# One subtraction issued a place earlier on VectorE, and four GpSimd operations behind one more wait, in the 512-step scan of a four-phase kernel

## What is computed

```
i_couple = tanh(q) @ coupling.T
dq = q - q ** 3 / 3.0 - p + drive + i_couple + bias
dp = EPSILON * (q + ALPHA - BETA * p)
dq1, dp1 = _derivative(q, p, ...)
dq2, dp2 = _derivative(q + 0.5 * DT * dq1, p + 0.5 * DT * dp1, ...)
dq3, dp3 = _derivative(q + 0.5 * DT * dq2, p + 0.5 * DT * dp2, ...)
dq4, dp4 = _derivative(q + DT * dq3, p + DT * dp3, ...)
q_next = clip(q + DT / 6.0 * (dq1 + 2 * dq2 + 2 * dq3 + dq4))
p_next = clip(p + DT / 6.0 * (dp1 + 2 * dp2 + 2 * dp3 + dp4))
```

## Time and profile before

| | |
|---|---|
| median of 3 runs | 5410.8 us (5400.78 to 5411.15) |
| profiled execution, its own time | 5413.09 us |
| its span, first to last instruction | 5411.5 us |
| mean granted TensorE clock over the span | 0.712 |
| TensorE products busy | 4425.1 us (82%) |
| VectorE busy | 4190.9 us (77%) |
| ScalarE busy | 2313.5 us (43%) |
| GpSimd busy | 1674.5 us (31%) |
| scan: first clip of q to the last | 45.67 to 2891.76 us |

### The profile page before, as it was taken

How to read it: one execution, slowest core, us unless ns; L and a number is a source line. 1 busy time by engine, 2 the same in 40 slices (tenths; PEclk the granted TensorE clock), 3 DMA queues, 4 the chain that set the end, 5 groups by cost and what they waited for, 6 DMA issues and landing times. The chain is left out here.

```text
span 5411.5 us, 212004 instructions
## 1 busy us (share of the span) xinstructions
PE 4425.1 (82%) x78665; PEld 3826.1 (71%) x78665; DVE 4190.9 (77%) x25454; ACT 2313.5 (43%) x10538; POOL 1674.5 (31%) x5965
## 2 busy tenths in 40 slices
PE   6977777777777777777776878699999999879899
PEld 5966666666666666666665666587777787668777
DVE  8999999999999999999995667677777777631123
ACT  3343333333333333333333656555555555432243
POOL 2444444444444444444443222223332222100000
PEclk5555555555555555555556999799999999989999
DMA  2000000000000000000002010222222222141121
GB/s 95 27 1 1 1 1 1 1 1 1 1 1 1 1 1 1 1 1 1 1 1 80 9 44 17 87 75 67 86 86 78 82 75 68 34 148 39 52 90 39
DMA packets 147685, 188.32 MB, mean 35 GB/s; under 512 B 9148, under 2 KB 79364, under 8 KB 147112
## 3 DMA queue, kind: packets, MB, share of 16 engines
q1 hardware_dynamic: 145712, 182.66, 10.2%
q0 software_dynamic: 624, 0.75, 0.1%
q10 hardware_dynamic: 904, 0.15, 0.0%
HBM read 143.66 MB, written 39.90 MB: 34 GB/s over the span
## 5 line engine op out<-in xcount | busy, mean ns | idle before, releaser
L249 PE MATMUL bank<-tanh_parts,w_lo 128*128 128x4 f16 x32768 | 1208.4, 169 | 679.3 <-ACT tanh_parts L189 679.3
L249 PEld LDWEIGHTS bank<-tanh_parts,w_lo 128*128 128x128 f16 x32768 | 1035.4, 105 | 855.2 <-ACT tanh_parts L189 853.9
L189 ACT ACTIVATE tanh_parts<-ys 128x8 f16<-128x8 f32 x4096 | 861.6, 210 | 1760.4 <-DVE ys L347 1760.4
L257 PE MATMUL bank<-tanh_parts,w_hi 128*128 128x8 f16 x32768 | 1212.6, 173 | 2.0 <-issue 2.0
L257 PEld LDWEIGHTS bank<-tanh_parts,w_hi 128*128 128x128 f16 x32768 | 1066.4, 104 | 7.7 <-issue 2.1
L347 DVE TENSOR_TENSOR_SCAN ys<-mix,bank 128x24 f32<-128x24 f32 x4096 | 820.8, 202 | 105.7 <-PE bank L257 2.2
L190 ACT ACTIVATE tanh_full<-ys 128x8 f32<-128x8 f32 x4096 | 805.0, 197 | 0.0
L337 DVE TENSOR_TENSOR tanh_parts<-tanh_full,tanh_parts 128x8 f16<-128x8 f32 x4096 | 679.5, 166 | 1.6 <-ACT tanh_full L190 1.6
L1246 POOL TENSOR_TENSOR t_w_qk<-t_raw_qk,t_w_qk 128x512 fp32r<-128x512 f32 x128 | 168.0, 1334 | 710.1 <-ACT t_w_qk L1410 710.1
L515 PE MATMUL t_bank<-t_x,t_w_qk 128*128 128x512 f32 x1536 | 360.9, 391 | 12.8 <-DVE t_x L1666 12.8
L515 PEld LDWEIGHTS t_bank<-t_x,t_w_qk 128*128 128x128 f32 x1536 | 289.6, 189 | 73.8 <-DVE t_x L1666 13.5
(11 more groups left out here) (232 smaller groups left out, 9143.4 us busy)
## 6 DMA issues: line engine op xcount, KB each, us to landing
t_raw_qk<-L_cond_qkv_w_dram SPq DMA_DIRECT2D x128, 256.0 KB, 3.3
t_raw_vo<-L_cond_qkv_w_dram SPq DMA_DIRECT2D x16, 1024.0 KB, 5.2
t_raw_vo<-L_cond_out_w_dram SPq DMA_DIRECT2D x16, 1024.0 KB, 5.2
n<-t_parts SPq DMA_DIRECT2D x14, 1024.0 KB, 6.6
g_raw<-L_cond_ffn_w_dram SPq DMA_DIRECT2D x8, 1024.0 KB, 10.1
g_x<-n SPq DMA_DIRECT2D x8, 1024.0 KB, 11.8
xT<-L_cond_ada_w_dram SPq DMA_DIRECT2D x8, 768.0 KB, 5.4
t_x<-n SPq DMA_DIRECT2D x6, 1024.0 KB, 7.0
```

The costliest lines, as they stand in the source:

```text
L189: act.activation(tanh_parts[:, u, at, :, 0], ys[:, s, at, :, 2], ACT.Tanh, scale=1.0 / SCALE).then_inc(s_th, 1)
L249: pe.matmul(sums[:, :, 2], w_lo[:, w_of, k, m * P:(m + 1) * P], tanh_parts[:, u, k, :, 0], start=(m % 2 == 0 and k == 0), stop=False, skip ...
L257: last = pe.matmul(sums[:, :, 1:3], w_hi[:, w_of, k, m * P:(m + 1) * P], tanh_parts[:, u, k], start=False, stop=(m % 2 == 1 and k == C - 1 ...
```

## The change

VectorE's low part of half 1 in the last stage is issued in front of `slope` in place of behind it. GpSimd gets one more wait in front of the first of its four operations: beside the clip of q it waits for the rate of stage 0. No instruction that computes is added or taken away.

```diff
@@ -424,8 +424,8 @@
                 own("rate_3", stt(rate[:, 3], ps_[:, 3], -BETA, y3))
                 cubed(y3, GAIN[3])
                 low_part(t, 3, 0)
+                low_part(t, 3, 1)
                 sloped(y3, THIRD + GAIN[3])
-                low_part(t, 3, 1)
                 v.wait_ge(s_psum, t + 1)
                 own("moved", stt(p_new[:, :, :], rate[:, 3], EPSILON * H / 3, p_sum[:, :, :]))
                 after("slope")
@@ -475,6 +475,7 @@
                 g.wait_ge(s_p, t + 1)
                 tt(net[:, :, :], drive_now[:, :, :], p[:, :, :], ALU.subtract).then_inc(s_net, 1)
                 g.wait_ge(s_clip, t + 1)
+                g.wait_ge(s_rate, t * 3 + 1)
                 own(tt(gq[:, 0], q[:, :, :], by_rest, ALU.mult))
                 g.wait_ge(s_net, t + 1)
                 of_net = own(tt(gq[:, 1], net[:, :, :], by_third_h, ALU.mult))
```

## The result

The changed kernel takes **5361.4 us** (median of 4 runs, 5358.1 to 5365.6), the kernel before 5411.0 beside it (4 runs). The ratio is 0.9913, with a 95% interval of 0.9896 to 0.993: 50 us, or 0.9%, faster. Forecast were 5357 us and a range of 5338 to 5390.

What follows compares the result with a forecast made beforehand. No engine's busy time was the bound; waits between engines were, costing time in stages 3 and 0. Gains averaging 0.105 us per step over 512 steps, 54 us, gave 5357 us, range 5338 to 5390.

Steps and rivals of the forecast that it cites:

- The two places: Stages 3 and 0 of a step, said to lose 0.09 and 0.06 us against stage 2 before the first scan.
- Stage 3, 0.08 in A and 0.02 in B: Moving the low part ends TensorE's pause in stage 3; the first scan comes sooner by these us, then held by `base`.
- A and B: Step kinds: in B, one in four, GpSimd's drive copy is late behind the loop's branch; A is the other three.
- Stage 0, 0.04: With GpSimd's wait, `mix` in stage 0 runs alone, 0.18 us for 0.22, and the first scan comes 0.04 us sooner.
- The sum: Whole step: 0.12 us gained in three of four steps, 0.06 in the fourth, mean 0.105, times 512 = 54 us.
- the margin of stage 1: Stage 1: 0.05 us free before the 5th high product is due, taken to cover one meeting with GpSimd's moved operations.
- The recorded bound of 0.06: Stage 1: upper cost per step, in us, of GpSimd's four operations in their new place; the forecast took nothing.
- The way to GpSimd, 0.15: Stage 0: time in us from the rate's end on VectorE to the start of `gq[:, 0]`, read from `net`.
- the near tie of `gq[:, 1]` and `p_1`: Stage 1: `p_1` starts 0.02 us second and is lengthened, making half 1's scan 0.08 late; rival at 5377 us, chance 0.33.
- The length of a meeting: Where VectorE and GpSimd operations overlap, the VectorE one starting second ends 0.01 to 0.04 us behind the GpSimd one.
- Rival 2: Stage 1: all four GpSimd operations lengthen VectorE's chain by 0.06 us each; slower, 5465 us, chance 0.05.
- Rivals 3 and 4: Stage 3 gains nothing, 5390 us, chance 0.05; or both stages reach TensorE's bound, 5342 us, chance 0.07.

Runs made afterwards that it cites:

- e1: Kernel before with only stage 3's low part of half 1 moved in front of the slope: 5378.7 us, ratio 0.9940.
- e2: Kernel before with only GpSimd's new wait for the rate of stage 0: 5391.2 us, ratio 0.9959.
- e5: Changed kernel with one more GpSimd operation, its result unused, in front of the four: 5373.0 us, ratio 0.9920.
- e4: Changed kernel with a further wait, for a count long reached, in front of GpSimd's four operations: 5363.7 us, ratio 0.9906.
- e3: Kernel before with GpSimd's copy of the next step's drive issued between two of its operations in stage 2: 5418.4 us, ratio 1.0009.
- e6: Kernel before with GpSimd's copy into trace issued behind `thirds` in place of in front, no new wait: 5391.6 us, ratio 0.9961.
- e7: Changed kernel with stage 3's `cub` before the rate, slope between low parts, `base` before `moved`, next drive's copy in stage 2, one added VectorE wait: 5380.2 us.
- e9: Same reordering and added wait as e7 on the changed kernel, but the copy of the next drive in stage 1: 5361.8 us, ratio 0.9908.
- e12: Changed kernel with one additional VectorE wait in front of `moved`, for the rate, long done there: 5371.6 us, ratio 0.9924.

## Why the prediction was right

- **The two places.** Right: nothing else in a step changed, and e1 and e2 give the two shares separately.
- **Stage 3, 0.08 in A and 0.02 in B.** The mechanism was right (the whole pause gone, `base` late next, A and B alike), the size a little high. Forecast were 0.065 in the mean, e1 measured 0.057: some 0.07 in A and 0.01 in B. The term that was off is `base`: the slope came 0.085 behind low part 1 in place of 0.08 and the rest of the chain some ns late, so the distance is 0.42 and not 0.41.
- **Stage 0, 0.04.** Right; e2 measured 0.047, the distance is 0.41 where I had 0.42.
- **The sum.** 0.105 forecast, 0.100 measured, 51 us over 511 steps; the median moved by 50 and not 54. The forecast's condition, that stage 1 gives nothing back, held, but not for the reason given, and that was partly luck. I had written that the margin of stage 1 covers one meeting; in e5 one meeting (0.066, at `known`) cost 0.03 per step. Nothing was lost because the four operations, sooner than I had them, met nothing that mattered. With the way at 0.17 (e4) the loss is 0.009 in the mean. The recorded bound of 0.06 was also added wrongly: two meetings of 0.05, less 0.05, plus 0.02 are 0.07.
- **The way to GpSimd, 0.15.** Wrong, and the one way in the sum that was. I took it from `net`, which waits for p by an instruction of its own. In front of `gq[:, 0]` it is the wait for the clip of q that got an instruction of its own, long done, and the wait for the rate sits on the operation: 0.08, as in all single waits. So the near tie of `gq[:, 1]` and `p_1`, on which I had put a third of the chances, did not take place. e4 brought it about at 0.01, and there `p_1` goes first; at the 0.02 of the prediction no run has `p_1`. The slope that I had called a won tie was none: its recorded start is up to 0.006 in front of that of `gq[:, 1]`.
- **The length of a meeting.** Right in form. The operation that starts second ends 0.02 to 0.04 behind the other: also `known` in e5 (1503.76 and 1503.73) and the rate in e3 (1501.42 and 1501.39). The exception is a near tie, where VectorE can still go first although its record starts behind, by 0.01 (`p_1` in e4) or up to 0.025 (`known_0` in e4). The Trainium skill ("SBUF — State Buffer", section "SBUF: two separate sides") has VectorE operations with two SBUF inputs and GpSimd operations exclude each other for the whole instruction, whichever starts first. The trace agrees on the exclusion and its length; the recorded start alone doesn't tell the winner of a near tie.
- **Rival 2.** Not seen. Even e5, built to meet, lost 0.03 per step, far from the 0.135 from which it decides.
- **Rivals 3 and 4.** Neither. The first scan of stage 3 did come sooner (0.49 to 0.42), and neither stage reached the 0.40 that TensorE allows.

## What to carry to other kernels

Where operations of two engines exclude each other, one on an engine with idle time can hold up the critical path of the other (0.04 to 0.06 us for each of the two meetings here): find the busy engine's lengthened operations by comparing the means of one shape at several places, and then move the other engine's operation, by order (e6) or by a wait (the change). Then look at what it meets in its new place, as e3 shows. Behind a wait, the order of two waits is worth as much as an operation, and so is one more instruction in each step of an unrolled program: a wait that orders nothing new cost 10 us here.

## What I had not expected of the hardware

- Two waits in front of one instruction: 0.10 us from the releaser's end when the one that has its own instruction is released last, 0.04 on VectorE when it is the other. On GpSimd 0.15 and 0.08.
- The recorded starts don't tell who wins a near tie: `known_0` went first at up to 0.025 behind GpSimd's copy (e4), `mix` was held at 0.001 to 0.005 behind it (before).
- 512 more waiting instructions in VectorE's unrolled program brought 49 steps of 460 that are up to 0.37 us longer, in the same steps in e7 and e9 and nearly the same in e12, and again every 128 steps.
- The first step of the scan took 7.7 to 10.9 us in the profiled executions of this study, so up to 3 us between two of them say nothing of the change.
